# Layer 3's attention taken two heads at a time, with turning over the full height, lengths in column groups and scores from half-height operands

## The chip, the cores and the metric

One core of a Trainium2 chip runs the whole kernel. The metric is the device time of one launch in microseconds (us), the median of three runs. TensorE (PE) multiplies, VectorE (DVE), ScalarE (ACT) and GpSimd (POOL) work on elements, SyncE (SP) issues most transfers. PSUM has 8 banks of 128 partitions x 512 float32.

## The reference, cut to what matters

Four layers, each `x = x + s * silu(ffn(xn))` with an attention `s` of its own, on 8 sequences of 512 tokens of width 128. Layer 3's attention, in complex numbers, 16 heads of 64 components:

```python
qr = q * phase; kr = k * phase            # turned by position, real and imaginary parts
s = einsum('bihd,bjhd->bhij', qr, conj(kr)).real
qn, kn = |q|^2 , |k|^2 summed over d      # lengths
maha = maximum(qn + E*E*kn - 2*E*s, 0) / V
logits = coef * log1p(maha / nu) + ...    # causal
out = softmax(logits) @ v ; y = out @ Wo
```

`E` and `V` depend on the distance i - j and the head alone.

## The kernel before

All layers are float32. The last stage, the "heads" stage, is layer 3's attention. A unit g is one head of one sequence (`UNITS` = 128; sequence g % 8, head g // 8). Each engine has its own program: a loop over u, and in it a fixed list of steps of units u to u+3 (`heads_pe`, `heads_dve`, `heads_act`, `heads_pool`). Semaphores (`after`, `piece`) tie the engines together; each engine takes its list strictly in order. For a unit, with i, x for query and key:

- PE `project` puts the query (bank 2) and the key (bank 3) into PSUM, 128 partitions = 64 real parts over 64 imaginary parts. DVE `cosines` multiplies each with the cosines, `sines` (two instructions, each from one half of the partitions into the other) with the sines, POOL `rotate` adds. ACT `square` squares the projections out of PSUM; PE `norms` sums the squares over the partitions with eight matmuls of one column, and ACT `norms` copies the 8 columns. POOL `norms` makes diagonal blocks `dk` from the key's lengths.
- PE `scores` fills bank 4 or 5 in three pieces (512; 384; 256 and 128 columns: causal blocks): a product of the 128-partition query and key, and one matmul with `dk` for each 128x128 block. DVE `query_norms`, `distance`, `logits`, with ACT `logarithm` and `exponential` between, make the weights in SBUF (`y`). PE `flip` transposes them, ACT `turned` copies them, PE `values` multiplies, ACT `outputs` scales, POOL `accumulate` adds into `acc`. PE `project_values` and ACT `values` make the values.
- SP `heads_loads` fetches weights, cosines and sines (`turn`) and tables (`tb`) of the head after the next. `heads_close` multiplies `acc` with the gate (DVE), adds and stores, a sequence at a time.

A float32 matmul of the program is two MATMUL records, a transpose is one. Nearly all matmuls are recorded at line 75 (`mm`), transposes at line 79 (`tr`), the DVE's scalar_tensor_tensor at line 83 (`stt`). `cosines` is line 3254, `sines` 3264, `logits` 3298, ACT `square` 3343 and 3347, POOL `rotate` 3442, `accumulate` 3449.

Layer 0 (`l0_pe`, `scores`) has, for four groups g of 32 partitions, in the order 0, 2, 1, 3, two matmuls each:

```python
for g in (0, 2, 1, 3):
    rows = slice(32 * g, 32 * g + 32)
    ...
    for pair in range(2):
        m = k.mm(sc[:, g // 2, col:col + P], t["qx"][rows, ...], kT[rows, ...], start=False)
```

Groups 0 and 2 write different banks and do not wait for each other; 1 and 3 wait for 0 and 2.

## Time and profile before

| | |
|---|---|
| three runs | 3187.17, 3195.63, 3196.6 us; median 3195.63 |
| span of the profiled execution | 3186.6 us; no time of its own beyond the span is given |
| PE, DVE, ACT, POOL busy | 96%, 75%, 57%, 27% of the span |
| heads stage | from about 1614 us to the end |

Busy is the time in which an engine has an instruction under way; PE's matmuls overlap, so that its rhythm is read from starts, not from the length of one matmul.

### The profile page before, as it was taken

To read this page: it belongs to the slowest core of one execution; us is meant where nothing else is said; L and a number is where in the kernel's file an instruction comes from. 1 tells how busy PE (TensorE), PEld (TensorE's weight loads), DVE (VectorE), ACT (ScalarE), POOL (GpSimd) and SP (SyncE) were. 2 spreads that over 40 slices of the span, in tenths; PEclk is the share of its full clock that TensorE was granted. 3 is DMA by queue.
4 is the path that set the end of the run, shared out by engine and by line. 5 is a ranking of instruction groups with operands and counts; after the bars stand their busy time and mean duration, and the time that the engine had idled before them with its cause. 6 is when DMAs were issued, how large, how long until landed. Compare 5 with 4: busy or idle time off the path is not lost. (4 is left out here: it accounts for less than half of the span.)

```text
span 3186.6 us, 57933 instructions
## 1 busy us (share of the span) xinstructions
PE 3070.1 (96%) x20342; PEld 2412.7 (76%) x20342; DVE 2384.5 (75%) x5016; ACT 1831.2 (57%) x4246; POOL 856.5 (27%) x707
## 2 busy tenths in 40 slices
PE   6999998999999999997899999999999999999998
PEld 5777675666666678785778888888888888888887
DVE  5878776565566555556868888888888888888888
ACT  3455543654655444433756666666666666666666
POOL 2111101100100100002423344443434444343443
PEclk9999998999999999998999999999999999999999
DMA  2000101000000000003001100011100110000100
GB/s 56 2 5 36 45 27 50 1 1 1 1 1 1 1 1 1 1 1 81 1 1 23 23 9 16 21 23 23 23 9 16 21 23 23 10 23 14 23 1 27
DMA packets 43554, 53.08 MB, mean 17 GB/s; under 512 B 8645, under 2 KB 27272, under 8 KB 43272
## 3 DMA queue, kind: packets, MB, share of 16 engines
q1 hardware_dynamic: 39298, 47.02, 5.9%
q8 instruction: 168, 2.75, 0.4%
q10 hardware_dynamic: 3974, 2.37, 0.3%
q14 instruction: 114, 0.93, 0.1%
HBM read 38.63 MB, written 10.75 MB: 15 GB/s over the span
## 5 line engine op out<-in xcount | busy, mean ns | idle before, releaser
L75 PE MATMUL banks<-scratch 128*128 128x128 f32 (+3 forms) x3648 | 715.7, 325 | 11.5 <-ACT scratch L2999 8.9
L75 PEld LDWEIGHTS banks<-scratch 128*128 128x128 f32 x3648 | 482.9, 192 | 77.0 <-issue 60.3
L75 PE MATMUL banks<-lower 128*128 128x128 f32 (+2 forms) x2688 | 506.7, 354 | 1.2 <-DMA lower<-in_L_w2T 0.6
L75 PEld LDWEIGHTS banks<-lower 128*128 128x128 f32 (+1 forms) x2688 | 343.1, 193 | 165.9 <-issue 164.7
L75 PEld LDWEIGHTS banks<-scratch,tb 128*128 128x128 f32 x2560 | 356.6, 191 | 102.1 <-issue 61.7
L75 PE MATMUL banks<-scratch,tb 128*128 128x128 f32 x2560 | 368.5, 275 | 0.0
L3442 POOL TENSOR_TENSOR scratch<-scratch,aT 128x1024 f32<-128x1024 f32 x128 | 358.8, 2803 | 4.5 <-DVE aT L3264 4.5
L83 DVE SCALAR_TENSOR_TENSOR scratch<-scratch,tb 128x512 f32<-128x512 f32 (+3 forms) x512 | 340.1, 706 | 8.4
L3434 POOL TENSOR_TENSOR scratch<-backwards,nn 128x512 f32<-128x512 f32 x128 | 133.3, 1042 | 736.2 <-ACT nn L3354 736.2
L83 DVE SCALAR_TENSOR_TENSOR scratch<-tb,nn,banks 128x512 f32<-128x512 f32 (+3 forms) x512 | 267.8, 544 | 75.8 <-PE banks L75 71.7
L3264 DVE TENSOR_TENSOR aT<-banks,turn 64x1024 f32<-64x1024 f32 x256 | 312.9, 1222 | 5.7
L3377 ACT ACTIVATE scratch<-banks 128x384 f32<-128x384 f32 (+1 forms) x384 | 200.0, 521 | 182.9 <-PE banks L79 182.9
L75 PE MATMUL banks<-nT,w 128*128 128x512 f32 x544 | 282.1, 602 | 3.0 <-DVE aT L3264 1.6
L3368 ACT ACTIVATE scratch<-scratch,mn 128x512 f32<-128x512 f32 (+3 forms) x512 | 282.8, 566 | 0.4 <-DVE mn L3298 0.2
L3254 DVE TENSOR_TENSOR scratch<-banks,turn 128x512 f32<-128x512 f32 x256 | 176.5, 690 | 138.3 <-PE banks L75 137.1
L3298 DVE CUSTOM_DVE_ANT_0 scratch<-scratch,tb,coef 128x512 f32<-128x512 f32 (+3 forms) x512 | 261.8, 549 | 0.0
L75 PEld LDWEIGHTS banks<-minus_half,sT 128*128 128x128 f32 x2048 | 239.2, 192 | 2.0 <-ACT sT L3347 2.0
L75 PE MATMUL banks<-minus_half,sT 128*128 128x1 f32 x2048 | 236.4, 245 | 1.2 <-ACT sT L3343 1.2
L79 PEld LDWEIGHTS banks<-ident,scratch 128*128 128x128 f32 x1408 | 171.0, 141 | 72.2 <-issue 69.6
L1474 DVE TENSOR_TENSOR lower<-lower,banks 128x512 f32<-128x512 f32 x160 | 109.0, 686 | 155.7 <-ACT lower L1687 155.5
L79 PE MATMUL banks<-ident,scratch 128*128 128x128 f32 x1408 | 219.2, 273 | 2.1 <-ACT scratch L3368 1.4
L3360 ACT ACTIVATE scratch<-scratch 128x384 f32<-128x384 f32 (+1 forms) x384 | 215.4, 562 | 8.0 <-DVE scratch L83 6.4
(422 smaller groups left out, 4957.1 us busy)
## 6 DMA issues: line engine op xcount, KB each, us to landing
tb<-head_rows SPq DMA_DIRECT2D x32, 512.0 KB, 7.0
turn<-head_turns SPq DMA_DIRECT2D x64, 128.0 KB, 2.7
head_turns<-loads SPq DMA_DIRECT2D x16, 256.0 KB, 2.8
head_turns<-rotation SPq DMA_DIRECT2D x16, 256.0 KB, 3.2
xs<-in_x SPq DMA_DIRECT2D x8, 256.0 KB
w<-in_L_Wqk SPq DMA_DIRECT2D x16, 128.0 KB, 2.0
out<-xs SPq DMA_DIRECT2D x8, 256.0 KB, 2.3
lower<-in_L_w3T ACTq DMA_DIRECT2D x1, 1280.0 KB, 9.2
```

What stands on the lines that cost most here:

```text
L75: return self.T.matmul(out, lhsT, rhs, start=start, stop=stop, skip_group_check=True)
L79: return self.T.matmul(out, in_, self.ident[0:n, 0:n], start=start, stop=True, is_transpose=True, skip_group_check=True)
L83: return self.V.scalar_tensor_tensor(out, a, s, b, op0, op1)
L1474: V.tensor_tensor(k.hidden[:, e % 2, m, b * S:(b + 1) * S], k.gated_h[:, m, :], k.bank(2 * m + 1), ALU.mult).then_inc(*k.l1_hid[m].up())
L3254: V.tensor_tensor(t["qk"][:, i * S:(i + 1) * S], k.bank(2 + i), hd["turn"][:, 0, :], ALU.mult).then_inc(*(k.h_ck if i else k.h_cq).up())
L3264: x = V.tensor_tensor(k.sines[there, :].rearrange("p (i s) -> p i s", i=2), k.bank(2, 2)[here, :, :], hd["turn"][here, 1, :].unsqueeze(1). ...
L3298: x = V.tensor_tensor_reduce(y, y, view(hd["tb"][:, 2, i * P + 127:i * P + 128], [[-1, n]]), k.coef[:, h:h + 1], 3e38, ALU.add, ALU.min, t ...
L3360: A.activation(y, y, ACT.Ln, bias=1.0).then_inc(*k.h_ln.up())
L3368: x = A.activation(y, y, ACT.Exp, bias=t["mn"][:, i:i + 1], scale=-1.0, accum_out=t["sum"][:, i:i + 1])
L3377: A.activation(t["pt"][:, lo:hi], k.bank(7 if piece == 1 else 6)[:, 0:hi - lo], ACT.Identity).then_inc(*k.h_pt.up())
L3434: G.tensor_tensor(t["dk"][:, :, :], k.backwards[:, :].unsqueeze(1).broadcast_to([P, 4, P]), t["nn"][:, 4:8].unsqueeze(2).broadcast_to([P, ...
L3442: G.tensor_tensor(t["qk"], t["qk"], k.sines, ALU.add).then_inc(*k.h_rot.up())
```

## The change

A step m is now two neighbouring heads (e = 0, 1) of one sequence (`PAIRS` = 64). A projected block holds the real parts of both heads (64 partitions each), another the imaginary parts, so that turning needs no move between partitions: one DVE instruction multiplies both blocks with the cosines, one with the sines, and POOL subtracts and adds. The squares are taken from the turned parts in SBUF. The lengths come from four matmuls with a stationary operand of 32 columns, each into its own 32 partitions of bank 2, a copy by ACT, and four matmuls that sum and transpose. The scores of head e use partitions 64e to 64e+63, real and imaginary part in two products, head e in bank 4 + e. Pieces are ordered 512; 256 and 128; 384. All four lists are new, `y` has four buffers in place of two, and weights, turns and tables are loaded for two heads at once.

```diff
+        k.norm_w = k.sb("norm_w", [P, 32])
+        k.fill(k.norm_w[:, :], 0.0)
+        k.fill(k.norm_w[0:64, 0:1], -0.5)
+        k.fill(k.norm_w[64:128, 1:2], -0.5)
...
-                       tb=k.sb(f"tb3_{j}", [P, 4, 512])) for j in range(2)]
+        k.squares = [t[:, :].rearrange("p (i s) -> p i s", i=2) for t in (k.sT, k.hT)]
+        k.sines = [t.rearrange("p (i s) -> p i s", i=2)
+                   for t in (k.aT[:, :], k.normed.rearrange("p t d -> p (t d)"))]
+        k.lengths = k.w1s.rearrange("p g h -> p (g h)")
+        k.norm_s = k.sb("norm_s", [P, 4])
+        k.pairs3 = [dict(qk=flat[:, 2048 * j:2048 * j + 2048].rearrange("p (x i s) -> p x i s", x=2, i=2),
+                         nn=k.sb(f"nn3_{j}", [P, TPB, 4])) for j in range(2)]
...
+            Y.wait_ge(k.h_pq.sem, done)
             Y.wait_ge(k.h_pk.sem, done)
-            Y.wait_ge(k.h_pq.sem, done)
-            k.load_weights(h)
+            k.load_weights(hp)
+            Y.wait_ge(k.h_ck.sem, done)
             Y.wait_ge(k.h_cq.sem, done)
-            Y.wait_ge(k.h_ck.sem, done)
-            Y.wait_ge(k.h_sin.sem, done)
-            k.load_turns(h)
-            Y.wait_ge(k.h_sc.sem, 3 * done)
-            Y.wait_ge(k.h_lg.sem, 3 * done)
-            k.load_tables(h)
-
-
-
-
+            Y.wait_ge(k.h_sinq.sem, done)
+            Y.wait_ge(k.h_sink.sem, done)
+            k.load_turns(hp)
+            Y.wait_ge(k.h_sc.sem, 6 * done)
+            Y.wait_ge(k.h_lg.sem, 6 * done)
+            k.load_tables(hp)
 
...
-        def project(g, i):
-            b, h, t, hd = k.unit(g)
+        def project(m, x):
+            if not 0 <= m < k.PAIRS:
+                return
+            b, hp, r, hd = k.pair(m)
+            if b == 0 and x == 0:
+                T.wait_ge(k.h_wt[hp % 2].sem, 80 * (hp // 2 + 1))
+            if x:
+                k.after(T, k.h_sinq, m + 1)
+            else:
+                k.after(T, k.h_nn, m)
+            for i in range(2):
+                t = k.mm(k.bank(2 + i), hd["w"][:, 2 * x + i, :], k.nT3[:, b, :])
+            t.then_inc(*(k.h_pk if x else k.h_pq).up())
+
+        def norms(m):
+            if not 0 <= m < k.PAIRS:
+                return
+            k.after(T, k.h_sinq, m + 1)
+            k.after(T, k.h_sink, m + 1)
+            k.after(T, k.h_sq, m + 1)
+            k.after(T, k.h_sk, m + 1)
+            for i in range(4):
+                t = k.mm(k.bank(2)[32 * i:32 * i + 32, :], k.norm_w[:, :], k.squares[i // 2][:, i % 2, :])
+            t.then_inc(*k.h_nl.up())
+
+        def sums(m):
+            if not 0 <= m < k.PAIRS:
+                return
+            k.after(T, k.h_nc, m + 1)
+            for i in range(TPB):
+                t = k.mm(k.bank(3)[:, 4 * i:4 * i + 4], k.lengths[:, i * P:(i + 1) * P], k.norm_s[:, :])
+            t.then_inc(*k.h_nnp.up())
+
+        def scores(m, p):
+            if not 0 <= m < k.PAIRS:
+                return
+            b, hp, r, hd = k.pair(m)
+            k.after(T, k.h_rot, 2 * (m + 1))
+            k.after(T, k.h_dk, 2 * (m + 1))
             if b == 0:
-                T.wait_ge(k.h_wt[h % 2].sem, 80 * (h // 2 + 1))
-            k.after(T, k.h_sin, g)
-            k.after(T, k.h_ck if i else k.h_cq, g)
-            k.mm(k.bank(2 + i), hd["w"][:, i, :], k.nT3[:, b, :]).then_inc(*(k.h_pk if i else k.h_pq).up())
-
...
-                T.wait_ge(k.h_tb[h % 2].sem, 32 * (h // 2 + 1))
-            k.piece(T, k.h_qn, "qn", (2, 1, 0)[piece], g + (piece == 2))
+                T.wait_ge(k.h_tb[hp % 2].sem, 64 * (hp // 2 + 1))
+            k.after(T, k.h_qn, k.pieces(m, p, 0) - 1)
             at = 0
-            for i in k.PIECES[piece]:
+            for i in k.PIECES[p]:
                 n = (i + 1) * P
-                ps = k.bank(5 if piece == 1 else 4)[:, at:at + n]
-                k.mm(ps, t["qk"][:, i * P:(i + 1) * P], t["qk"][:, S:S + n], stop=False)
+                for x in range(2):
+                    for e in range(2):
+                        rows = slice(64 * e, 64 * e + 64)
+                        k.mm(k.bank(4 + e)[:, at:at + n], r["qk"][rows, 0, x, i * P:(i + 1) * P],
+                             r["qk"][rows, 1, x, 0:n], start=(x == 0), stop=False)
+                for e in range(2):
+                    dk = k.lanes3[(2 * m + e) % 4]["dk"]
+                    for j in range(i + 1):
+                        t = k.mm(k.bank(4 + e)[:, at + j * P:at + (j + 1) * P],
+                                 hd["tb"][:, e, 3, (i - j) * P:(i - j + 1) * P], dk[:, 3 - j, :], start=False)
+                    if i == k.PIECES[p][-1]:
+                        t.then_inc(*k.h_sc.up())
+                at += n
+
...
+        for m in range(-4, k.PAIRS + 1):
+            values(2 * m - 1, 2)
+            scores(m + 1, 2)
+            norms(m + 2)
+            values(2 * m, 0)
+            flip(2 * m + 1, 0)
+            sums(m + 2)
+            project_values(2 * m + 1)
+            flip(2 * m + 1, 1)
+            project(m + 3, 0)
+            values(2 * m, 1)
+            values(2 * m, 2)
+            flip(2 * m + 1, 2)
+            scores(m + 2, 0)
+            project(m + 3, 1)
+            flip(2 * m + 2, 0)
+            values(2 * m + 1, 0)
+            flip(2 * m + 2, 1)
+            scores(m + 2, 1)
+            flip(2 * m + 2, 2)
+            values(2 * m + 1, 1)
+            project_values(2 * m + 2)
...
-        def cosines(g, i):
-            b, h, t, hd = k.unit(g)
+        def products(m, x, i):
+            if not 0 <= m < k.PAIRS:
+                return
+            b, hp, r, hd = k.pair(m)
             if b == 0:
-                V.wait_ge(k.h_wt[h % 2].sem, 80 * (h // 2 + 1))
-            k.after(V, k.h_sc, 3 * (g - 1))
+                V.wait_ge(k.h_wt[hp % 2].sem, 80 * (hp // 2 + 1))
+            k.after(V, k.h_pk if x else k.h_pq, m + 1)
             if i:
-                k.after(V, k.h_sk, g + 1)
+                k.after(V, k.h_rot, 2 * m + x)
+                V.tensor_tensor(k.sines[x], k.bank(2, 2), hd["turn"][:, 1, :].unsqueeze(1).broadcast_to([P, 2, S]),
+                                ALU.mult).then_inc(*(k.h_sink if x else k.h_sinq).up())
             else:
-                k.after(V, k.h_pq, g + 1)
-            V.tensor_tensor(t["qk"][:, i * S:(i + 1) * S], k.bank(2 + i), hd["turn"][:, 0, :],
-                            ALU.mult).then_inc(*(k.h_ck if i else k.h_cq).up())
-
-        def sines(g):
-            b, h, t, hd = k.unit(g)
-            k.after(V, k.h_sq, g + 1)
-            k.after(V, k.h_sk, g + 1)
-            k.after(V, k.h_rot, g)
-            for i in range(2):
-                here, there = slice(64 * i, 64 * i + 64), slice(64 - 64 * i, 128 - 64 * i)
-                x = V.tensor_tensor(k.sines[there, :].rearrange("p (i s) -> p i s", i=2), k.bank(2, 2)[here, :, :],
-                                    hd["turn"][here, 1, :].unsqueeze(1).broadcast_to([64, 2, S]), ALU.mult)
-            x.then_inc(*k.h_sin.up())
-
...
-            if b == 0:
...
+                k.after(V, k.h_sc, 6 * (m - 1))
+                k.after(V, k.h_sk if x else k.h_sq, m - 1)
+                V.tensor_tensor(r["qk"][:, x, :, :], k.bank(2, 2), hd["turn"][:, 0, :].unsqueeze(1).broadcast_to([P, 2, S]),
+                                ALU.mult).then_inc(*(k.h_ck if x else k.h_cq).up())
+
...
+        for m in range(-4, k.PAIRS + 1):
+            distance(2 * m + 2, 1)
+            logits(2 * m + 2, 0)
+            logits(2 * m + 3, 0)
+            distance(2 * m + 3, 1)
+            reciprocals(2 * m)
+            query_norms(2 * m + 2, 2)
+            logits(2 * m + 2, 1)
+            query_norms(2 * m + 3, 2)
+            distance(2 * m + 2, 2)
+            logits(2 * m + 3, 1)
+            distance(2 * m + 3, 2)
+            logits(2 * m + 2, 2)
+            products(m + 3, 0, 0)
+            logits(2 * m + 3, 2)
+            products(m + 3, 0, 1)
+            query_norms(2 * m + 4, 0)
+            query_norms(2 * m + 5, 0)
+            distance(2 * m + 4, 0)
+            products(m + 3, 1, 0)
+            products(m + 3, 1, 1)
+            reciprocals(2 * m + 1)
+            query_norms(2 * m + 4, 1)
+            distance(2 * m + 5, 0)
+            query_norms(2 * m + 5, 1)
...
-            k.piece(A, k.h_y, "y", piece, g + 1)
-            y = t["y"][:, (0, 512, 896)[piece]:(512, 896, 1280)[piece]]
+        def square(m, x):
+            if not 0 <= m < k.PAIRS:
+                return
+            b, hp, r, hd = k.pair(m)
+            k.after(A, k.h_rot, 2 * m + x + 1)
+            k.after(A, k.h_nl, m)
+            out = view(k.squares[1][:, 0, S - 1:S], [[S, 2], [-1, S]]) if x else k.squares[0]
+            A.activation(out, r["qk"][:, x, :, :], ACT.Square).then_inc(*(k.h_sk if x else k.h_sq).up())
+
+        def lengths(m):
+            if not 0 <= m < k.PAIRS:
+                return
+            k.after(A, k.h_nl, m + 1)
+            k.after(A, k.h_nnp, m)
+            A.activation(k.lengths, k.bank(2), ACT.Identity).then_inc(*k.h_nc.up())
+
+        def norms(m):
+            if not 0 <= m < k.PAIRS:
+                return
+            b, hp, r, hd = k.pair(m)
+            k.after(A, k.h_nnp, m + 1)
+            k.after(A, k.h_dk, 2 * (m - 1))
+            k.after(A, k.h_qn, 6 * (m - 1))
+            A.activation(r["nn"].rearrange("p i c -> p (i c)"), k.bank(3)[:, 0:16], ACT.Identity).then_inc(*k.h_nn.up())
...
+        for m in range(-4, k.PAIRS + 1):
+            square(m + 2, 0)
+            turned(2 * m, 2)
+            logarithm(2 * m + 3, 0)
+            values(2 * m)
+            square(m + 2, 1)
+            outputs(2 * m - 1)
+            logarithm(2 * m + 2, 1)
+            lengths(m + 2)
+            logarithm(2 * m + 3, 1)
+            exponential(2 * m + 2, 0)
+            norms(m + 2)
+            logarithm(2 * m + 2, 2)
+            values(2 * m + 1)
+            turned(2 * m + 1, 0)
+            exponential(2 * m + 3, 0)
+            exponential(2 * m + 2, 1)
+            logarithm(2 * m + 3, 2)
+            outputs(2 * m)
+            turned(2 * m + 1, 1)
+            exponential(2 * m + 3, 1)
+            turned(2 * m + 1, 2)
+            logarithm(2 * m + 4, 0)
+            exponential(2 * m + 2, 2)
+            turned(2 * m + 2, 0)
+            turned(2 * m + 2, 1)
+            exponential(2 * m + 3, 2)
...
+        def rotate(m, x):
+            if not 0 <= m < k.PAIRS:
+                return
+            b, hp, r, hd = k.pair(m)
+            k.after(G, k.h_ck if x else k.h_cq, m + 1)
+            k.after(G, k.h_sink if x else k.h_sinq, m + 1)
+            A, B = r["qk"][:, x, 0, :], r["qk"][:, x, 1, :]
+            G.tensor_tensor(A, A, k.sines[x][:, 1, :], ALU.subtract)
+            G.tensor_tensor(B, B, k.sines[x][:, 0, :], ALU.add).then_inc(*k.h_rot.up())
...
+        for m in range(-4, k.PAIRS + 1):
+            rotate(m + 2, 0)
+            rotate(m + 2, 1)
+            accumulate(2 * m - 2)
+            accumulate(2 * m - 1)
+            norms(2 * m + 4)
+            norms(2 * m + 5)
```

## Rows read from the trace of the kernel before

**Rows 1.** The page, busy time of the engines over the span

```profile
PE 3070.1 (96%) x20342; PEld 2412.7 (76%) x20342; DVE 2384.5 (75%) x5016; ACT 1831.2 (57%) x4246; POOL 856.5 (27%) x707
```

**Rows 2.** Busy time by stretch, 124 units: length, PE, PEld, DVE, ACT, POOL

```profile
1652.00:3156.00 1504.00, 1504.00 (x10677) 1280.63 (x10676) 1290.83 (x2606) 999.35 (x2735) 626.45 (x374) 1.00 0.08 17
```

**Rows 3.** The chain that ended last: start, length; first and last of 124 beats

```profile
1645.40 4.88 PE banks L75 x38
...
3135.64 4.88 PE banks L75 x38
```

**Rows 4.** Timeline of PE in the heads stage: start, length from first to last end

```profile
2399.88 1.58 PE L75 MATMUL banks<-scratch 128*128 128x128 f32 x12
...
2401.30 0.60 PE L79 MATMUL banks<-ident,scratch 128*128 128x128 f32 x4
...
2408.53 1.02 PE L75 MATMUL banks<-scratch 128*128 128x512 f32 x2
2409.39 1.05 PE L75 MATMUL banks<-scratch,tb 128*128 128x128 f32 x8
2410.28 1.84 PE L75 MATMUL banks<-minus_half,sT 128*128 128x1 f32 x16
2411.99 0.47 PE L75 MATMUL banks<-scratch 128*128 128x128 f32 x2
```

**Rows 5.** Timeline of PE in layer 0, around matmuls of 64 partitions

```profile
290.65 2.05 PE L75 MATMUL banks<-scratch,pt 128*128 128x128 f32 x16
292.54 0.59 PE L75 MATMUL banks<-mask_rest,identb 128*128 128x512 bf16 x2
...
295.99 0.60 PE L79 MATMUL banks<-ident,p 128*128 128x128 f32 x4
296.52 1.98 PE L75 MATMUL banks<-scratch,wo 64*128 64x512 f32 x4
298.43 1.05 PE L75 MATMUL banks<-scratch,pt 128*128 128x128 f32 x7
```

**Rows 6.** Timeline of PE in layer 2, around a stationary operand of 64 columns

```profile
1019.32 1.93 PE L75 MATMUL banks<-upper,wg 128*64 128x512 f32 x4
1021.18 0.71 PE L75 MATMUL banks<-lower 128*128 128x128 f32 x4
```

**Rows 7.** Timeline of PE, layer 0 scores: 154.78 to 154.80, then to 155.5

```profile
154.78 0.39 PE L75 MATMUL banks<-kT,qx 32*128 32x128 f32 x2
...
154.78 0.72 PE L75 MATMUL banks<-kT,qx 32*128 32x128 f32 x8
```

**Rows 8.** Groups by line and shape, 1600 to 3180: busy, mean ns, idle before

```profile
L3264 DVE TENSOR_TENSOR aT<-banks,turn 64x1024 f32<-64x1024 f32 x256 | 312.9, 1222 | 5.7
L3254 DVE TENSOR_TENSOR scratch<-banks,turn 128x512 f32<-128x512 f32 x256 | 176.5, 690 | 138.3 <-PE banks L75 137.1 <-ACT sT L3343 1.2
L3343 ACT ACTIVATE sT<-banks 128x512 f32<-128x512 f32 x128 | 75.8, 592 | 0.5 <-PE banks L75 0.4
```

**Rows 9.** Timeline of DVE and POOL in two units of the heads stage

```profile
2415.03 1.63 DVE L83 SCALAR_TENSOR_TENSOR scratch<-scratch,tb 128x512 f32<-128x512 f32 x1
2416.69 0.74 DVE L83 SCALAR_TENSOR_TENSOR scratch<-tb,nn,banks 128x256 f32<-128x256 f32 x2
...
2414.84 1.28 POOL L3449 TENSOR_TENSOR acc<-acc,scratch 128x512 f32<-128x512 f32 x1 [1.37 <-ACT scratch L3392]
2416.07 2.81 POOL L3442 TENSOR_TENSOR scratch<-scratch,aT 128x1024 f32<-128x1024 f32 x1
...
3161.40 0.69 DVE L83 SCALAR_TENSOR_TENSOR scratch<-scratch,tb 128x512 f32<-128x512 f32 x1
```

**Rows 10.** Timeline of the stage's first projections and scores, and its last accumulate

```profile
1614.05 1.96 PE L75 MATMUL banks<-nT,w 128*128 128x512 f32 x4 [1.37 <-PEq L69]
...
1623.97 1.80 PE L75 MATMUL banks<-scratch 128*128 128x512 f32 x2
...
3177.95 1.75 POOL L3449 TENSOR_TENSOR acc<-acc,scratch 128x512 f32<-128x512 f32 x1 [5.58 <-ACT scratch L3392]
```

More of the change, by code:

```diff
@@ new lines, in scores, with flip @@
+                for e in range(2):
+                    dk = k.lanes3[(2 * m + e) % 4]["dk"]
[5 more added lines that the diff above has]
+                at += n
+        def flip(g, p):
+            if not 0 <= g < k.UNITS:
+                return
+            m, e, t, r, hd = k.unit(g)
+            f = 3 * g + p
+            k.after(T, k.h_exp, k.pieces(m, p, e))
+            k.after(T, k.h_pt, f - 1)
+            at = 0
+            for i in k.PIECES[p]:
+                for j in range(i + 1):
+                    x = k.tr(k.bank(6 + f % 2)[:, at:at + P],
@@ L3275, in query_norms @@
+        def query_norms(g, p):
+            if not 0 <= g < k.UNITS:
+                return
+            m, e, t, r, hd = k.unit(g)
+            k.after(V, k.h_sc, k.pieces(m, p, e))
+            k.after(V, k.h_nn, m + 1)
+            if m % SEQS == 0:
+                V.wait_ge(k.h_tb[m // SEQS % 2].sem, 64 * (m // SEQS // 2 + 1))
+            k.after(V, k.h_fl, 3 * (g - 4) + p + 1)
             at = 0
-            for i in k.PIECES[piece]:
+            for i in k.PIECES[p]:
                 n = (i + 1) * P
-                x = k.stt(t["y"][:, k.AT[i]:k.AT[i] + n], view(hd["tb"][:, 0, i * P + 127:i * P + 128], [[-1, n]]),
-                          t["nn"][:, i:i + 1], k.bank(5 if piece == 1 else 4)[:, at:at + n], ALU.mult, ALU.add)
+                x = k.stt(t["y"][:, k.AT[i]:k.AT[i] + n], view(hd["tb"][:, e, 0, i * P + 127:i * P + 128], [[-1, n]]),
+                          r["nn"][:, i, e:e + 1], k.bank(4 + e)[:, at:at + n], ALU.mult, ALU.add)
@@ L3290, in distance, with logits @@
             x.then_inc(*k.h_y.up())
-        def logits(g, piece):
-            b, h, t, hd = k.unit(g)
-            k.piece(V, k.h_ln, "ln", piece, g + 1)
-            for i in k.PIECES[piece]:
+        def logits(g, p):
+            if not 0 <= g < k.UNITS:
+                return
+            m, e, t, r, hd = k.unit(g)
+            h = 2 * (m // SEQS) + e
+            k.after(V, k.h_ln, k.pieces(m, p, e))
+            for i in k.PIECES[p]:
                 n = (i + 1) * P
                 y = t["y"][:, k.AT[i]:k.AT[i] + n]
-                x = V.tensor_tensor_reduce(y, y, view(hd["tb"][:, 2, i * P + 127:i * P + 128], [[-1, n]]),
+                x = V.tensor_tensor_reduce(y, y, view(hd["tb"][:, e, 2, i * P + 127:i * P + 128], [[-1, n]]),
@@ new lines, in reciprocals @@
+            if not 0 <= g < k.UNITS:
+                return
+            m, e, t, r, hd = k.unit(g)
+            k.after(V, k.h_exp, k.pieces(m, 2, e))
+            k.after(V, k.h_out, g - 3)
+            V.reciprocal(t["rs"][:, :], t["sum"][:, :]).then_inc(*k.h_rs.up())
+        for m in range(-4, k.PAIRS + 1):
[23 more added lines that the diff above has]
+            query_norms(2 * m + 5, 1)
@@ new lines, in logarithm, with exponential @@
+        def logarithm(g, p):
+            if not 0 <= g < k.UNITS:
+                return
+            m, e, t, r, hd = k.unit(g)
+            k.after(A, k.h_y, k.pieces(m, p, e))
+            y = t["y"][:, k.SPAN[p][0]:k.SPAN[p][1]]
+            A.activation(y, y, ACT.Ln, bias=1.0).then_inc(*k.h_ln.up())
+        def exponential(g, p):
+            if not 0 <= g < k.UNITS:
+                return
+            m, e, t, r, hd = k.unit(g)
+            k.after(A, k.h_lg, k.pieces(m, p, e))
+            k.after(A, k.h_rs, g - 3)
+            for i in k.PIECES[p]:
```

315 lines of the change are left out of this document (94 added, 221 removed).

## The prediction

> **What bounds the kernel now.** I read the page's busy times first: PE has work under way for 96% of the span and no other engine for more than 75% [rows 1]. A busy share does not make PE the bound by itself, so I went to the busy times by stretch. Over 1504 us in the middle of the heads stage PE is never idle, DVE is busy for 86% of it, ACT for 66%, POOL for 42% [rows 2]. The chain that ended last then shows what sets the rhythm: the same piece of PE work comes back from 1645.40 to 3135.64, 123 beats, so 1490.24 / 123 = 12.116 us for a unit, 24.23 us for two [rows 3]. Within the stage this chain is PE alone. So the change is worth what it does to PE's row of starts, as long as nobody else comes in late; DVE has 12.116 - 0.86 x 12.116 = 1.7 us of room a unit.
>
> PE's prices are read between starts [rows 4]. Twelve halves of 128 columns take 1.42 us when they follow the one-column matmuls; eight take 0.89 us (2409.39 to 2410.28), 0.111 each. Two halves of 512 columns take 0.86, 0.43 each. Sixteen one-column halves (one unit's lengths) take 1.71, and the first matmul behind them another 0.08 (1.42 - 12 x 0.111): 1.79 us, as long as sixteen full ones, because each brings its own 128-column stationary operand.
>
> **The change on PE, for two units.** Values, blocks with dk, values' projection, transposes and projections keep number and width, and so their time.
>
> Lengths, removed: 2 x 1.79 = 3.58 us.
>
> Lengths, added: four matmuls of 512 columns, eight halves. No row shows two column groups at work together. Bounds: all four together, two halves long, 2 x 0.43 = 0.86; one after another, 8 x 0.43 = 3.44. I take 0.86, because the nearest rows, two row groups, do run together. The first two matmul records of layer 0's scores start within 0.02 us of each other, and eight halves over groups 0 and 2 are over in 0.72 us [rows 7] where eight full ones take 1.05 [rows 4]. The two records are not two halves of one matmul in turn: they are groups 0 and 2, though the program puts all four halves of group 0 first.
>
> Sums, added: four matmuls with 128-column stationary operands and four columns, eight halves at 0.111 = 0.89 us.
>
> Scores: each product of 128 partitions becomes two of 64, for two heads. Run as above, each head's stream is 512 columns x 4 halves beside the other's: 4 x 0.43 = 1.72, what two units took before. The smaller pieces scale alike. Change 0; bound above, if the heads did not overlap, one more full set of 1280 columns x 4 halves, 4.3 us.
>
> Changing the shape of the array, added. This has a price of its own in every stretch where it happens. Four transposes before a 64-partition group take 0.53 us instead of 4 x 0.11: 0.09 late. The four halves of 512 columns then take 1.91 instead of 1.72: 0.10 late in front and 0.09 at the exit. Sixteen full halves behind such a group take 1.89 instead of 1.78: 0.10 late [rows 5]. Together 0.38 us for a round trip. A stationary operand of 64 columns pays too: four halves in 1.86 instead of 1.72, 0.05 and 0.09 [rows 6], so fewer columns only shorten the part in front. The new list of a step makes four round trips for scores (piece 512; 256; 128; 384, each with its dk blocks between) and one for lengths: 4 x 0.38 + (0.09 + 0.03 + 0.09 + 0.10) = 1.83 us. The cost is nothing only if the array's change hid behind other matmuls; none of the samples does that.
>
> PE in all: 24.23 - 3.58 + 0.86 + 0.89 + 1.83 = 24.23 us. What the lengths give, the shape changes take.
>
> **The other engines.** DVE before: per two units four `sines` of 1.22 and four `cosines` of 0.69, 7.6 us; now four products of 1024 columns over 128 partitions, 1.22 each from the 64-partition row, 4.9 us [rows 8]. DVE falls from 20.8 to some 18 us in 24.2. ACT: four squares of 0.59 become two of 1024 columns, near 1.0 each, and one more copy of 0.59: +0.2 us [rows 8]. POOL's rotation is the same amount in four pieces. SP: half the turn transfers, the same table bytes, each awaited a whole head pair (8 x 24 = 194 us) ahead; the waits of `heads_loads` hold only later loads. All this lies beside PE and costs nothing while PE stays ahead; in front of the stage the three fills of `norm_w`, the one DVE add before `meet` and 2 more head tables cost well under 1 us.
>
> **Where someone comes late.** I walked the new lists by hand, putting PE's prices end to end. Projection, products, rotation, squares, lengths, copy, sums, copy before the next `project` use banks 2 and 3 in turn; each handoff has 0.5 us or more to spare. One has not. `scores(m+1, 2)` waits until `query_norms` has read both heads' 256/128 piece. From head 0's last dk block PE has 2 halves of head 1, three transposes, six halves of values, eight of values' projection, six of values: 22 x 0.111 + 3 x 0.109 = 2.8 us. A matmul's result comes about 0.16 after its slot (1.58 - 1.42 us for the twelve of rows 4), and the two handoffs some 0.04 each, leaving 2.5. In it DVE does `query_norms` 0.74, `distance(2m+5, 0)`, `query_norms` 0.74. `distance` of 512 columns lasts 0.69 alone: 2.2, in time. But started beside POOL's `accumulate` it lasts 1.63: it began 0.2 into a POOL instruction of 1.28 us and ended 0.5 after it [rows 9]. By my walk POOL ends the second rotation about 0.5 before this `distance` and goes straight to an `accumulate` whose input is long ready. Then DVE needs 2.5 to 3.5 us, and PE waits 0 to 0.9. I take 0.4. Behind PE's wait stand lengths, values and the next projections, so the whole step moves: 64 x 0.4 = 26 us.
>
> Ends of the stage: before, first projection to first scores took 9.9 us [rows 10]; the longer chain of a head pair takes about 18, +8. At the end, before, 6.9 us of the span lie behind the last `accumulate` (3177.95 + 1.75 to 3186.6) [rows 10], several closing steps queued in them; now all but the last sequence's run under the last pairs' work, which I estimate at 4 less. Sum +4.
>
> **Sum.** Against the profiled execution: 3186.6 + 0 + 26 + 4 = 3216.6. The three runs lie 0.6 to 10 above that span, the median 9.0; I add the change to the median: 3195.6 + 30 = 3226 us. By 0.3%, about what a measurement of this kernel tells from no change, the border is 9.6 us.
>
> **A rule against it.** In layer 0, groups 0 and 2 start side by side although group 0's four halves come first in the program [rows 7]. The Trainium skill ("TensorE: Matmul & The Clock Gate", part 3 on packing small matmuls) says that matmuls start and end strictly in program order. By that rule the two halves of one matmul hold up the next group, and each set takes five halves' time instead of four (scores) or two (lengths).
>
> **The rivals.**
> (a) No wait: the `accumulate` falls beside the distance. 3195.6 + 4 = 3200. For: 0.3 us of room alone. Against: POOL's list.
> (b) More waits: the same mechanism at other distances and logits, 1.0 to 1.5 us a step: 3264 to 3296. For: POOL is busy 42% of the time [rows 2], and `distance` and `logits` both have two operands in SBUF. Against: before, POOL made one `distance` a unit 0.94 us longer (1.63 for 0.69) and PE lost nothing by it [rows 2, 9].
> (c) Column groups strictly one after another: +2.58 x 64 = +165, 3391. For: no row shows groups of columns together. Against: row groups do.
> (d) Groups overlap only in order: lengths 5 x 0.43 instead of 0.86, +1.29, x 64 = +83: 3309; with scores too (one half more in each of 512, 384, 256, 128 columns, 0.43 + 0.32 + 0.22 + 0.11 = 1.08), +152: 3378. For: nothing in the rows. Against: rows 7 for row groups.
> (e) Faster: the array's change is cheaper in this dense stream, because two streams give a load of weights something to hide behind. PE loses 3.58 - 1.75 = 1.83 us a step if it costs nothing: 24.23 - 1.83 = 22.4, 3195.6 - 117 + 4 = 3083; at half price 3141, and DVE's wait, tied to PE's own work, stays. It decides once the five round trips cost together under 1.2 us (1.83 less 0.4 less 0.2), 0.24 each instead of 0.37. For: rows 7's eight halves with two streams still show 0.10 in front, but hide nothing else. Against: every sample of rows 5 and 6.
>
> **Chances.** The forecast (wait of 0.2 to 0.8 us) 0.38, (a) 0.17, (b) 0.14, (c) 0.07, (d) 0.06, (e) 0.18. The forecast's own range is 3212 to 3252. For 8 in 10 I reach down to half price in (e), 3141, and up to (b) and the first of (d), 3312. Faster is (e), 0.18; within 0.3% is (a), 0.17; slower the rest, 0.65.
>
> **What would show it.** Right: between starts of the same step about 24.6 us; the lengths' eight halves begun within about 1.1 us; 0.2 us gaps in PE's starts at each change of shape; a wait of PE in front of the 64-partition matmuls of 384 columns, ended by DVE line 83; `distance` of 512 columns over 1.2 us there. Wrong: lengths of 3.4 us (c); a second head's matmul starting only after the first head's (d); steps of 23 us or less, with DVE or PE's changes invisible (e); waits in other places (b).

## The result, and the profile after

| kernel | runs | median us | lowest to highest | profiled run, span |
|---|---|---|---|---|
| before | 4 | 3194.81 | 3187.17 to 3196.6 | span 3186.6 |
| after | 4 | 3220.43 | 3211.66 to 3221.64 | 3220.42, span 3219.0 |

The ratio is 1.0078, 95% interval 1.0056 to 1.0100: the change makes the kernel 0.8% slower, 25.6 us by the medians. The forecast was +30 us, of which 26 was to be a wait in every step and 4 the ends of the stage. The sum came out; its parts did not.

The page's busy times after stand against [rows 1]:

```profile
PE 3090.7 (96%) x20342; PEld 2273.3 (71%) x20342; DVE 2174.1 (68%) x4761; ACT 1817.7 (56%) x4118; POOL 838.8 (26%) x838
```

By stretch, 1400 us in the middle of the heads stage (length, PE, PEld, DVE, ACT, POOL, granted clock, DMA share, GB/s), first after, then before:

```profile
1700.00:3100.00 1400.00, 1399.90 (x9903) 1056.37 (x9902) 1004.93 (x2194) 913.69 (x2412) 562.99 (x460) 1.00 0.06 14
```

```profile
1700.00:3100.00 1400.00, 1400.00 (x9932) 1191.34 (x9931) 1203.57 (x2428) 930.83 (x2544) 585.79 (x347) 1.00 0.08 18
```

DVE falls from 86% to 72% of the stretch and nothing comes of it: PE has work under way throughout in both, as it had in [rows 2]. The rhythm stands in the chain that ended last (start, length), the same piece of PE work at the two ends of 60 steps:

```profile
1703.13 7.34 PE banks L75 x56
...
3164.14 7.38 PE banks L75 x56
```

(3164.14 - 1703.13) / 60 = 24.350 us a step; before it was 24.232 (2 x 12.116, [rows 3]). That is +0.12 us a step, 64 x 0.12 = 8 us, where the forecast had 26.

The rest is outside the steps. From the first projection to the end of the span, before takes 3186.6 - 1614.05 = 1572.6 us and after 3219.0 - 1620.51 = 1598.5: +25.9, as much as the medians differ. Less 64 steps, 21.7 are left before and 40.1 after. I call this remainder "the ends" from here on; it grew by 18 where I had 4. The 6.5 us by which the stage begins later in this profile I count as scatter: in the profiled runs below the stage begins anywhere between 1605.9 and 1627.8, and the layers ahead are the same code.

One step of PE after (timeline: start, length from first start to last end), as [rows 4] show it before:

```profile
2410.52 0.83 PE L75 MATMUL banks<-n,pt 128*128 128x128 f32 x6
2411.37 1.56 PE L75 MATMUL banks<-scratch 64*128 64x384 f32 x8
2412.86 1.60 PE L75 MATMUL banks<-scratch,tb 128*128 128x128 f32 x12
2414.39 0.62 PE L75 MATMUL banks<-sT,norm_w 128*32 128x512 f32 x2
2414.41 0.62 PE L75 MATMUL banks<-hT,norm_w 128*32 128x512 f32 x2
2414.85 0.60 PE L75 MATMUL banks<-sT,norm_w 128*32 128x512 f32 x2
2414.86 0.60 PE L75 MATMUL banks<-hT,norm_w 128*32 128x512 f32 x2
2415.39 1.16 PE L75 MATMUL banks<-n,pt 128*128 128x128 f32 x8
...
2416.82 0.95 PE L75 MATMUL banks<-norm_s,w1s 128*128 128x4 f32 x8
2417.63 1.14 PE L75 MATMUL banks<-wvo,nT 128*128 128x128 f32 x8
...
2422.41 1.99 PE L75 MATMUL banks<-scratch 64*128 64x512 f32 x8
2424.33 2.05 PE L75 MATMUL banks<-scratch,tb 128*128 128x128 f32 x16
```

The lengths' eight halves start in two waves of four, 0.45 us apart, and the next matmul starts 1.00 us after the first (2415.39 - 2414.39): 0.86 of work and 0.14 of change. The sums take 0.81. Eight halves of 512 columns for two heads take 1.92 (2424.33 - 2422.41): 1.72 of work and 0.20 of change, and another 0.10 lies in front of the dk blocks behind. All of that is within 0.1 us of its price.

The forecast wait is in the first two lines. Six halves of values should take 6 x 0.111 + 0.09 for the change of shape = 0.76, and the 384 piece comes 0.85 later: PE is 0.09 late here, and 0.03 in the next step (2434.93 to 2435.72). DVE and POOL at this place:

```profile
2408.61 0.74 DVE L83 SCALAR_TENSOR_TENSOR scratch<-tb,nn,banks 128x256 f32<-128x256 f32 x2 [2.38 <-PE banks L75]
2409.27 1.31 DVE L83 SCALAR_TENSOR_TENSOR scratch<-scratch,tb 128x512 f32<-128x512 f32 x1
2410.49 0.73 DVE L83 SCALAR_TENSOR_TENSOR scratch<-tb,nn,banks 128x256 f32<-128x256 f32 x2
```

```profile
2407.52 1.27 POOL L3502 TENSOR_TENSOR scratch<-scratch,normed 128x512 f32<-128x512 f32 x1
2408.74 1.28 POOL L3514 TENSOR_TENSOR acc<-acc,moe 128x512 f32<-128x512 f32 x1
```

The collision is the one that was described: `distance` begins 0.53 into an `accumulate` of 1.28 and lasts 1.31 for 0.69 alone [rows 9]. But the DVE chain ends 2.61 us after it began (2411.22 - 2408.61), 0.1 over the 2.5 of room, at the bottom of the 2.5 to 3.5 that I gave it. In both kernels the lengthened `distance` ends some 0.55 us after the POOL instruction beside which it began: 2416.66 against 2416.12 in [rows 9], 2410.58 against 2410.02 here. It is shorter here because it began 0.53 into that instruction and not 0.19.

The start of the stage after (timeline of PE; in brackets the idle time in front and what ended it), against [rows 10]:

```profile
1620.51 1.96 PE L75 MATMUL banks<-nT,w 128*128 128x512 f32 x4 [1.37 <-PEq L69]
1624.99 3.52 PE L75 MATMUL banks<-nT,w 128*128 128x512 f32 x4 [2.52 <-DVE aT L3291]
1634.83 1.07 PE L75 MATMUL banks<-sT,norm_w 128*32 128x512 f32 x2 [6.33 <-ACT hT L3384]
...
1643.32 2.89 PE L75 MATMUL banks<-scratch 64*128 64x512 f32 x8
...
1656.28 2.93 PE L75 MATMUL banks<-scratch 64*128 64x384 f32 x8 [2.93 <-DVE scratch L83]
```

And the same start by stretch, after and then before:

```profile
1620.50:1680.90 60.40, 45.61 (x198) 25.35 (x198) 32.02 (x53) 17.70 (x38) 19.52 (x16) 0.77 0.00 1
```

```profile
1614.00:1641.80 27.80, 25.00 (x136) 18.19 (x136) 18.51 (x29) 10.20 (x23) 8.19 (x5) 0.88 0.00 1
1641.80:1700.00 58.20, 58.13 (x411) 49.40 (x412) 48.37 (x106) 38.05 (x104) 21.50 (x15) 1.00 0.01 4
```

Before, the first scores start 9.9 us after the first projection; after, 22.8. PE is idle for 60.40 - 45.61 = 14.8 us against 2.8, and while it works the granted clock is 0.77 for 60 us against 0.88 for 28. As an estimate from these rows, the clock costs 0.23 x 45.6 = 10.5 us against 0.12 x 25.0 = 3.0. Together 25 against 6: +12 of idle time and +7 to 8 of clock, 19 at the start.

The end of the stage, from the start of the last 384 piece, after and then before:

```profile
3187.22:3219.00 31.78, 20.29 (x155) 18.67 (x154) 20.41 (x42) 17.38 (x53) 7.00 (x5) 0.89 0.23 67
```

```profile
3163.99:3186.60 22.61, 8.71 (x66) 7.30 (x64) 15.28 (x31) 9.37 (x28) 3.06 (x3) 0.90 0.32 93
```

PE is idle for 11.5 us of it after and for 13.9 before; the clock costs, by the same estimate, 2.2 and 0.9. That is about -1 for the change.

### The profile page after: what moved, and what is told of

The parts are those of the page before. It is cut to its first block and busy times, and to the rows that moved or that the text cites. A ratio compares the mean times of both kernels' runs of the same rounds, so it can differ in the third digit from the quotient of the medians.

```text
span 3219.0 us, 56888 instructions
## 1 busy us (share of the span) xinstructions
PE 3090.7 (96%) x20342; PEld 2273.3 (71%) x20342; DVE 2174.1 (68%) x4761; ACT 1817.7 (56%) x4118; POOL 838.8 (26%) x838
## 5 line engine op out<-in xcount | busy, mean ns | idle before, releaser
L75 PE MATMUL banks<-scratch 64*128 64x256 f32 (+4 forms) x2112 | 363.9, 456 | 13.0 <-ACT scratch L3009 8.9
L75 PEld LDWEIGHTS banks<-n,pt 128*128 128x128 f32 x2560 | 316.5, 192 | 83.9 <-issue 83.9
L3336 DVE CUSTOM_DVE_ANT_0 scratch<-scratch,tb,coef 128x512 f32<-128x512 f32 (+3 forms) x512 | 323.9, 659 | 47.3 <-ACT scratch L3408 47.2
L75 PE MATMUL banks<-n,pt 128*128 128x128 f32 x2560 | 345.2, 278 | 2.3 <-ACT moe L3449 2.3
L3430 ACT ACTIVATE pt<-banks 128x384 f32<-128x384 f32 (+1 forms) x384 | 202.2, 528 | 125.5 <-PE banks L79 125.5
L83 DVE SCALAR_TENSOR_TENSOR scratch<-scratch,tb 128x512 f32<-128x512 f32 (+3 forms) x512 | 270.3, 548 | 0.0
L75 PEld LDWEIGHTS banks<-scratch 64*128 64x128 f32 (+1 forms) x2112 | 182.5, 187 | 104.2 <-issue 61.3
L3296 DVE TENSOR_TENSOR scratch<-banks,turn 128x1024 f32<-128x1024 f32 x128 | 156.8, 1225 | 126.3 <-PE banks L75 113.7
L3514 POOL TENSOR_TENSOR acc<-acc,moe 128x512 f32<-128x512 f32 x120 | 154.0, 1284 | 263.2 <-ACT moe L3449 263.2
L1691 ACT ACTIVATE lower<-banks 128x512 f32<-128x512 f32 x160 | 94.2, 597 | 199.4 <-PE banks L75 199.2
```

The costliest lines, as they stand in the source:

```text
L75: return self.T.matmul(out, lhsT, rhs, start=start, stop=stop, skip_group_check=True)
L83: return self.V.scalar_tensor_tensor(out, a, s, b, op0, op1)
L1691: A.activation(k.gated_h[:, m, :], k.bank(2 * m), ACT.Silu).then_inc(*k.l1_silu[m].up())
L3296: V.tensor_tensor(r["qk"][:, x, :, :], k.bank(2, 2), hd["turn"][:, 0, :].unsqueeze(1).broadcast_to([P, 2, S]), ALU.mult).then_inc(*(k.h_ck ...
L3336: x = V.tensor_tensor_reduce(y, y, view(hd["tb"][:, e, 2, i * P + 127:i * P + 128], [[-1, n]]), k.coef[:, h:h + 1], 3e38, ALU.add, ALU.min ...
L3430: A.activation(t["pt"][:, lo:hi], k.bank(6 + f % 2)[:, 0:hi - lo], ACT.Identity).then_inc(*k.h_pt.up())
```

## The experiments

Below, "step" is the distance of PE's beats, "stage" the time from the first projection to the end of the span, "ends" the stage less its steps, all from the profiled execution. The ends vary by 5 us among profiles of kernels that leave them alone (40.1 to 35.1; experiment 7 shows why); the beginning of the stage varies by 22, so the stage says more than the span does. A kernel's executions are scattered by up to 26 us, and the longer ones have the lower mean granted clock: in experiment 3, 3206.56 us at 0.975 and 3230.21 at 0.969.

**1. The changed kernel again.** No edit.

> The changed kernel again, on the chip of the next three, as their yardstick: 3220 us (3212 to 3222), steps of 24.35 us.

Measured: 3221.37 us (3219.89 to 3228.01) against 3192.94 for before on the same chip, ratio 1.0094 [1.0060, 1.0127]; step 24.351, stage 1598.4, ends 40.0. Both halves of the reading repeat.

**2. One round trip less.** The pieces 256 and 128 share a bank, so both heads' half-height products go first, and the dk blocks behind.

```diff
             for i in k.PIECES[p]:
+                at[i] = sum((j + 1) * P for j in k.PIECES[p][:k.PIECES[p].index(i)])
                 for x in range(2):
                     for e in range(2):
-                        k.mm(k.bank(4 + e)[:, at:at + n], ..., start=(x == 0), stop=False)
-                for e in range(2):
-                    ...
+                        k.mm(k.bank(4 + e)[:, at[i]:at[i] + n], ..., start=(x == 0 and at[i] == 0), stop=False)
+            for e in range(2):
+                for i in k.PIECES[p]:
+                    ...
```

> In the piece of 256 and 128 columns all half-height products come first and all dk blocks behind them, so that the array changes its shape one round trip less a step. Theory (PE sets the rhythm and a round trip costs it 0.38 us): steps of 23.97 us, 64 x 0.38 = 24 us less than the changed kernel, about 3196. Rival (somebody else's lateness sets the step, or the change of shape hides): no difference, 3220.

Measured: 3193.42 us (3185.31 to 3201.44, 10 runs), 28 below the changed kernel's 3221.37; against before 0.9996 [0.9976, 1.0016]. Step 23.925, 0.43 less. Its PE timeline:

```profile
2408.75 1.58 PE L75 MATMUL banks<-scratch 64*128 64x256 f32 x16
2410.26 1.61 PE L75 MATMUL banks<-scratch,tb 128*128 128x128 f32 x12
2411.70 0.49 PE L79 MATMUL banks<-ident,scratch 128*128 128x128 f32 x3
...
2413.59 0.83 PE L75 MATMUL banks<-n,pt 128*128 128x128 f32 x6
2414.35 1.56 PE L75 MATMUL banks<-scratch 64*128 64x384 f32 x8
```

The same two pieces in the changed kernel:

```profile
2405.28 1.13 PE L75 MATMUL banks<-scratch 64*128 64x256 f32 x8
...
2408.63 0.49 PE L79 MATMUL banks<-ident,scratch 128*128 128x128 f32 x3
```

The two pieces take 2.95 us (2411.70 - 2408.75) where the changed kernel has 3.35 (2408.63 - 2405.28): 0.40 for the trip priced at 0.38, 26 us in 64 steps. The 384 piece now comes 0.76 behind the values' six halves, so the small wait is gone too.

**3. Accumulate between the two rotations.** It takes away the collision of the forecast's main term.

```diff
             rotate(m + 2, 0)
-            rotate(m + 2, 1)
             accumulate(2 * m - 2)
+            rotate(m + 2, 1)
             accumulate(2 * m - 1)
```

> POOL's first accumulate of a step is moved between the two rotations, so that it no longer lies beside the distance of 512 columns in front of the 384-column scores. The recorded forecast priced that collision at 0.4 us of PE a step: then 26 us less, about 3195. What the changed kernel's trace shows (distance lengthened to 1.3 us, but PE late by 0.03 to 0.1 us only): 2 to 5 us less, about 3216.

Measured: 3217.49 us (3206.56 to 3230.21, 7 runs), 1.0079 [1.0055, 1.0104]; step 24.321, stage 1594.0. `distance` takes 0.68 us at this place again (at 2411.93), and the wait is gone in the timeline:

```profile
2413.19 0.83 PE L75 MATMUL banks<-n,pt 128*128 128x128 f32 x6
2413.95 1.56 PE L75 MATMUL banks<-scratch 64*128 64x384 f32 x8
```

0.76 between the two, and the step is shorter by 0.03: 2 us in 64 steps. So the wait that was to cost 26 us costs 2, and the other 0.09 of the step (24.321 - 24.232) is what my prices, taken together, fell short by.

**4. Lengths on the full array.** The column groups and the sums give way to 16 matmuls of two columns, 32 halves, each with its own 128-column stationary operand, in one row. The sums and ACT's copy in front of them are left out.

```diff
-            for i in range(4):
-                t = k.mm(k.bank(2)[32 * i:32 * i + 32, :], k.norm_w[:, :], k.squares[i // 2][:, i % 2, :])
+            for i in range(TPB):
+                for x in range(2):
+                    for c in range(2):
+                        t = k.mm(k.bank(3)[:, 4 * i + 2 * x:4 * i + 2 * x + 2],
+                                 k.squares[x][:, c, i * P:(i + 1) * P], k.norm_w[:, 0:2],
+                                 start=(c == 0), stop=(c == 1))
```

> The lengths from sixteen matmuls over the full array (squares stationary, two columns moving) straight into bank 3, without column groups, copy and sums. Theory (the four column groups run side by side: 1.19 us with their round trip, and 0.89 for the sums, against 32 x 0.111 + 0.08 = 3.64): steps longer by 1.56 us, +100 us, about 3320, less 2 for a shorter chain at the start. Rival (the columns are no gain): 3220.

Measured: 3421.48 us (3415.36 to 3426.07), 1.071 [1.0668, 1.0752]: 200 above the changed kernel, twice the 100 that the matmuls' own prices give and that I expected. Step 27.655, +3.30. The 32 halves take what they should, 3.49 us; what is behind them does not:

```profile
2404.97 0.51 PE L75 MATMUL banks<-norm_w,sT 128*128 128x2 f32 x4
...
2408.02 0.59 PE L75 MATMUL banks<-norm_w,hT 128*128 128x2 f32 x4
2408.46 1.14 PE L75 MATMUL banks<-n,pt 128*128 128x128 f32 x8
...
2410.03 1.91 PE L75 MATMUL banks<-wvo,nT 128*128 128x128 f32 x8
```

By stretch, the lengths, what follows, and the rest of the step:

```profile
2405.00:2409.40 4.40, 4.40 (x42) 4.40 (x41) 3.57 (x13) 1.49 (x5) 1.23 (x2) 1.00 0.02 4
2409.60:2413.50 3.90, 3.90 (x18) 3.31 (x16) 0.77 (x2) 1.52 (x3) 1.67 (x2) 0.56 0.00 0
2414.50:2420.00 5.50, 5.50 (x40) 4.10 (x39) 3.56 (x5) 3.32 (x13) 2.29 (x2) 1.00 0.00 0
```

After 32 almost empty halves the clock is granted at 0.56 for 3.9 us, that is mostly the lower level, 1.2 GHz for 2.4, with PE never idle; the eight `wvo` halves start over 1.71 us (to 2411.74) for 0.98 in the changed kernel. This was in neither theory; experiment 5 is about it.

**5. The same lengths in two places.** The first x's 16 halves stay, the second's stand where the sums stood. The matmuls are those of experiment 4.

```diff
-            norms(m + 2)
+            norms(m + 2, 0)
             values(2 * m, 0)
             flip(2 * m + 1, 0)
-            sums(m + 2)
+            norms(m + 2, 1)
```

> As the run with the lengths over the full array, but its 32 halves stand in two places of 16, with values and transposes between. That run came out 200 us slower, not 100: its trace shows steps of 27.65 us and a granted clock of 0.93 where the changed kernel has 1.00. Theory (the long stretch of nearly empty matmuls lets the clock fall, the work itself costs 1.56 us a step): clock back near 1.00, steps of 25.9 us, about 3320. Rival (the lengths over the full array cost 3.3 us a step by themselves): 3421 again.

Measured: 3316.78 us (3305.24 to 3317.95), 1.0378 [1.0360, 1.0396]; step 25.845. Granted clock in the steady stretch, and the two groups:

```profile
1700.00:3100.00 1400.00, 1399.90 (x10184) 1127.59 (x10183) 943.24 (x2056) 828.16 (x2221) 530.21 (x434) 1.00 0.06 14
```

```profile
2411.83 1.84 PE L75 MATMUL banks<-norm_w,sT 128*128 128x2 f32 x16
...
2414.95 1.84 PE L75 MATMUL banks<-norm_w,hT 128*128 128x2 f32 x16
```

The clock is back at 1.00 and 1.81 us a step with it (27.655 - 25.845), 116 us by the steps and 105 by the medians. So of the 200 us of experiment 4 about half is work and half is clock. What is shown is that the placing of the 32 halves decides it; no run tried another way to divide them. Against this way of doing lengths, the column groups and sums of the change save 25.845 - 24.351 = 1.49 us a step.

**6. Lengths straight behind the scores' half-height products.** On top of experiment 2, `norms` moves between the products of piece 384 and their dk blocks, so that the array goes from 64 partitions to 32 columns without being full between.

```diff
+            if p == 2:
+                norms(m + 1)
             for e in range(2):
                 dk = k.lanes3[(2 * m + e) % 4]["dk"]
...
-            norms(m + 2)
```

> As the run with one round trip less, and the lengths are issued between the half-height products of the 384-column piece and its dk blocks, so that the array goes from 64-partition to 32-column shape without the full shape between. Theory (each change of shape costs about 0.19 us): 0.19 + 0.38 us less a step than the changed kernel, 36 us less, about 3184. Rival (a direct change between two small shapes costs as much as two): 24 us less, 3196; or, if lengths issued earlier now wait for ACT's squares, slower than that.

Measured: 3174.26 us (3163.26 to 3179.88, 8 runs) against 3192.43 for before, 0.9940 [0.9918, 0.9962]: faster than before. Step 23.730, 0.195 under experiment 2.

```profile
2421.98 1.56 PE L75 MATMUL banks<-scratch 64*128 64x384 f32 x8
2423.47 0.62 PE L75 MATMUL banks<-sT,norm_w 128*32 128x512 f32 x2
...
2424.47 1.60 PE L75 MATMUL banks<-scratch,tb 128*128 128x128 f32 x12
2425.91 1.06 PE L75 MATMUL banks<-n,pt 128*128 128x128 f32 x8
```

Products 1.49, lengths 1.00, dk 1.44, values 0.89: 4.82 us, where experiment 2 has 1.49, 1.54, 1.00 and 0.99 for the same. The exit to the full array and the entry from it have become one direct change, and that change costs no more than either. In these streams the price goes by the number of changes. The median is 10 us under the 3184 expected, the step 0.05 under (23.78 expected), which is 3 of them; the rest is within the scatter of the medians (experiment 8, with the same step, has 3179).

**7. Half the heads.** Both kernels with 8 of the 16 heads, so that their outputs lack the other heads' share. A cost of the steps halves, a cost of the ends stays. The edit of the changed kernel, whose loads for the other heads go too (the kernel before has `UNITS` halved in the same way):

```diff
-    PAIRS = 8 * SEQS
+    PAIRS = 4 * SEQS
```

> The changed kernel with 8 of 16 heads in the last stage (32 steps instead of 64; the output lacks the other heads). It separates steps from ends. Steps of 24.35 us: 3220 - 779 = 2441. With the kernel before halved, the difference is 22 us if the ends cost 18.7 and the steps 0.115 each; 13 us if all of the loss lay in the steps.

> The kernel before with 8 of 16 heads in the last stage (64 units instead of 128; the output lacks the other heads). Units of 12.116 us: 3194.8 - 775.4 = 2419.

Measured: changed 2442.13 us (2430.33 to 2454.46), before 2416.07 (2412.37 to 2419.94): 26.1 apart, as far as with all heads. The stages are 814.2 and 797.2, 17.0 apart, the ends 35.1 and 21.7, 13.4 apart; steps are unchanged (24.346 and 24.232). With 18 us in the ends and 8 in the steps, half the heads should leave 18 + 4 = 22; with all of it in the steps, 13. The stages lie between the two and the medians above both.

The granted clock says why. Here is the stage up to the second step's 384 piece, the stretch of the changed kernel's 60.40 us above, in the halved kernel and in experiment 3, which do the same work up to there:

```profile
1622.10:1678.70 56.60, 41.73 (x200) 24.09 (x200) 32.40 (x53) 17.81 (x38) 19.51 (x16) 0.85 0.00 1
```

```profile
1627.80:1684.30 56.50, 41.67 (x198) 23.98 (x199) 32.38 (x53) 17.71 (x38) 19.51 (x16) 0.85 0.00 1
```

PE is idle for 14.8 or 14.9 us in all three, but the clock is granted at 0.85 and not at 0.77: by the estimate used above 0.15 x 41.7 = 6.3 us instead of 10.5, and the stretch is 3.9 shorter. The end of the stage, from the last 384 piece, is shorter too, 30.8 us for 31.8, at 0.98 for 0.89. With these 5 us of clock, which come and go under the same code, the stages differ by 17.0 + 4.9 = 21.9, where 22 was expected. So 18 us in the ends belong to the profiles at 0.77, about 13 to the halved one at 0.85, and either way most of the cost does not scale with the number of steps: in the stages their share is 32 x 0.114 = 3.6 us.

**8. Experiment 6 and 3 together.**

> Lengths beside scores, one round trip less, and the earlier accumulate together. If the prices add: 3220 - 36 - 4 = 3180, some 15 us faster than the kernel before. If DVE or ACT become what a step waits for (they are busy about 18 and 19 of the then 23.8 us): 3185 to 3200.

Measured: 3179.07 us (3162.67 to 3189.07, 9 runs), 0.9948 [0.9926, 0.9970]; step 23.730, exactly that of experiment 6. With the wait already gone, moving `accumulate` gives nothing. DVE and ACT stay ahead of PE; the 18 and 19 us of the expectation are too high, the changed kernel's stretch above gives 17.5 and 15.9 a step.

**9. The first two projections early.** It aims at the start: for the first two head pairs every projection gets banks of its own out of 2 to 7, which are still unused, so that none waits for the turning of the one before.

```diff
+    def early(self, m, x):
+        return ((2, 4), (6, 0))[m][x] if m < 2 else 2
...
-            if x:
-                k.after(T, k.h_sinq, m + 1)
-            else:
-                k.after(T, k.h_nn, m)
+            if m > 1:
+                k.after(T, k.h_sinq if x else k.h_nn, m + 1 if x else m)
...
+            if m + 3 == 0:
+                project(1, 0)
+                project(1, 1)
```

> The changed kernel, but the first two steps' four projections go to banks that are still free (2 and 3, 4 and 5, 6 and 7, 0 and 1) and are issued at once, so that they wait for no products or lengths. Theory (the changed kernel's loss outside its steps, 18 us more than before, lies in the start, where PE waits some 15 us for a chain through banks 2 and 3, part of it at half clock): stage 5 to 8 us shorter, steps unchanged at 24.35, about 3214. Rival (the loss lies at the end of the stage): no difference.

Measured: 3210.67 us (3206.75 to 3218.14) against 3192.51, 1.0050 [1.0033, 1.0066]; step 24.352, stage 1592.3, 6.1 less.

```profile
1624.37 7.11 PE L75 MATMUL banks<-nT,w 128*128 128x512 f32 x16 [1.37 <-PEq L69]
1636.65 1.07 PE L75 MATMUL banks<-sT,norm_w 128*32 128x512 f32 x2 [5.17 <-ACT hT L3392]
...
1643.60 3.78 PE L75 MATMUL banks<-scratch 64*128 64x512 f32 x8 [2.45 <-issue]
```

The wait of 2.5 for DVE is gone and the next projections fill part of the gap, but PE still waits 5.2 us for the squares, and the first scores start 19.2 us after the first projection instead of 22.8. The second step's 384 piece comes 54.5 us in, against 60.5 in the changed kernel, which is where the stage's 6 us are. About 4 of them need not be the edit's: the granted clock of that stretch is 0.84 here, and with the old start and the clock at 0.85 it took 56.5 (experiments 3 and 7). Against those, PE is idle for 13.6 us and not 14.8, and the piece comes 2 us earlier. That much I read as the edit's own. The medians differ by more, 10 us to the changed kernel's 3220.4 and 3221.4; whether the edit also raises the clock at the start can't be told from one profile of each kind.

**10. The same on experiment 6.**

> The same early projections in the kernel with the lengths beside the scores (3174 us, steps of 23.73): 5 to 8 us less, about 3167, some 25 us faster than the kernel before. Rival: no difference, 3174.

Measured: 3172.21 us (3164.61 to 3180.09, 6 runs) against 3192.51, 0.9931 [0.9915, 0.9948]; stage 1552.0 for 1555.9. The expectation was 3167, and a gain of 5 to 8 us is not shown: experiment 8, without the early projections, has a stage of 1551.6. It has the lowest median, 0.7% under before, but can't be told apart from experiment 6 (0.9940) by its time.

## Why the prediction was right in its total by luck and wrong in its terms

**What bounds it: right.** PE's row of starts sets the time in every version. DVE lost 14 points of busy share for nothing.

**PE's prices: right within 0.1 us in 24.** Lengths 0.86 and sums 0.89 were forecast, 0.86 and 0.81 came. The scores' two streams overlap in full. A round trip of the array's shape (to fewer partitions or columns and back) was 0.38, read off single samples in layers 0 and 2 [rows 5, 6]; taking one out gave 0.40 in the timeline, and joining two changes gave 0.195 (half of 0.38 is 0.19). The step without its wait is 24.32 against the forecast 24.23. Rival (e), shape changes cheaper in a dense stream, is refuted by the same numbers.

**Column groups: right.** Rivals (c) and (d) are refuted by the second wave of the lengths, 0.45 us after the first with all four groups in both, and by 1.92 us for eight halves of 512 columns where (d) needs 0.43 more. The Trainium skill's sentence ("TensorE: Matmul & The Clock Gate", part 3) that matmuls start and end strictly in program order is not what this trace shows between groups of rows or of columns, if the halves are issued in the order in which the program lists the matmuls. The records carry no place in the program, so that the order is taken from the kernel's text.

**The wait: the first step that failed.** "Then DVE needs 2.5 to 3.5 us, and PE waits 0 to 0.9. I take 0.4. Behind PE's wait stand lengths, values and the next projections, so the whole step moves: 64 x 0.4 = 26 us." Place, releaser and collision came as described, and `distance` lasted 1.31; PE was 0.03 to 0.09 late, and without the collision the kernel gained 0.03 a step. The room of 2.5 was right. My 0.4 stood for a DVE chain of 2.9 us; my own walk, with `distance` begun 0.5 into the `accumulate`, would have given 0.74 + 1.3 + 0.74 = 2.8. The three durations were 0.74, 1.31 and 0.73, 2.78 in all, so the stretched `distance` was 0.1 shorter than I took it; and back to back the next instruction starts 0.66 and 1.22 after the one before, some 0.08 less than its length each time, which makes it 2.61. Those 0.3 us, in 64 steps, are most of the term. The nearest to the truth among the rivals is (a), no wait, but its time of 3200 is also wrong, by the next term.

**The ends: the other step that failed.** "the longer chain of a head pair takes about 18, +8 [...] which I estimate at 4 less. Sum +4." It is +18. The chain took 22.8 instead of 18, and that was the smaller part. I priced the delay of the first scores alone. The chain comes again for the second pair, since both use banks 2 and 3 in turn, and PE, idle in short pieces, works at a granted clock of 0.77 for 60 us. I had no term for the clock. Of the 19 us at the start 12 are PE idle and 7 to 8 the clock; the idle time is the same 14.8 us in every profile of this start, the clock's part falls to 3 to 4 where it is granted at 0.85. Experiment 7 shows that the cost stays when half the steps go. The gain of 4 at the end of the stage came to about 1, by the two stretches above.

So the terms were: wait 26 forecast, 2 measured; ends 4 and 18; the step's prices 0 and 6 (0.09 x 64). The sums are 30 and 26. That the total came out is luck: one error of -24 met two of +14 and +6. The direction was right for the wrong main reason. What stays open is why the same start is granted 0.77 in two profiles and 0.85 in two others.

## What to carry to other kernels

On a stream that TensorE bounds, count the changes of array shape (partitions or columns in use) as items with a price, here 0.19 us each, and order the matmuls so that those of unlike shape stand together: the change as made was 0.8% slower than before, and the same operations with three changes fewer a step (experiment 6) are 0.6% faster. When steps get larger, price the fill of the pipeline too, up to the first step at full rhythm and with the clock that is granted there (0.77 and 0.85 here, 1.00 in the steps), not only the first result. And before believing a wait made of several back-to-back instructions, add their start-to-start distances, not their durations.

## What the runs showed of the hardware that was not expected

- A row of 32 halves with two columns each, back to back for 3.5 us, was followed by 3.9 us at a granted clock of 0.56 although TensorE was never idle; 16 of them in each of two places left it at 1.00. The difference is 1.81 us a step.
- The same start of the stage, with the same waits (PE idle 14.8 us), was granted a clock of 0.77 in two profiles and of 0.85 in two others, and was 3.9 us shorter in these.
- Going from 64 partitions straight to 32 columns cost what going to or from the full array cost, one change of about 0.19 us (experiment 6).
- DVE's `logits` (line 3336), with two operands in SBUF as `distance` has, was lengthened beside POOL as well: 0.98 us for 256 columns beside `accumulate`, 0.49 without it two microseconds later. The step shows no wait of PE for it.
- The layers ahead of the stage, the same code in all these kernels, ended between 1605.9 and 1627.8 us in the profiled executions.
